# Small attention stages: denominators from the context matmul, sorted by DMA, weighed on GpSimd, projected two steps later

## What is computed

```python
q = (layernorm(x) @ Wq.T + bq).reshape(B, S, 16, 8).transpose(0, 2, 1, 3)
k = (ctx @ Wk.T + bk).reshape(B, S, 16, 8).transpose(0, 2, 1, 3)
v = (ctx @ Wv.T + bv).reshape(B, S, 16, 8).transpose(0, 2, 1, 3)
scores = jnp.einsum('bhqd,bhkd->bhqk', q, k) / jnp.sqrt(8.0)
attn = softmax(where(mask == 0, -1e9, scores), axis=-1)
ctx = jnp.einsum('bhqk,bhkd->bhqd', attn, v).transpose(0, 2, 1, 3).reshape(B, S, 128)
x = x + tanh(g) * (ctx @ Wo.T + bo)
```

## Time and profile before

| | |
|---|---|
| Median of 3 runs | 1778.14 us |
| Lowest and highest | 1774.27 and 1782.25 us |
| Span of the profiled execution | 1775.3 us (its total time is not given apart) |
| TensorE busy in the span | 1625.8 us, 92% |
| VectorE, ScalarE, GpSimd busy | 62%, 52%, 31% |
| Layer 0's attention | about 17 to 226 us of the span |
| Layer 3's attention | about 1444 to 1650 us |

### The profile page before, as it was taken

The page is one execution under the profiler, slowest core; times in us unless marked ns, Lnnn a source line. Parts: engine busy times, 40 slices in busy tenths (PEclk is TensorE's granted clock), DMA queues, the critical chain, the costliest instruction groups (busy, mean ns, idle before and its releaser), DMA issues. The chain is left out here.

```text
span 1775.3 us, 50142 instructions
## 1 busy us (share of the span) xinstructions
PE 1625.8 (92%) x19432; PEld 1110.8 (63%) x19432; DVE 1092.4 (62%) x2384; ACT 924.1 (52%) x2277; POOL 547.2 (31%) x968
## 2 busy tenths in 40 slices
PE   3999989899999999987987799979999978999898
PEld 1666654577777777764775456646777755666454
DVE  4677767566666666645156788862223236778686
ACT  3666526455656565533444566534334346665354
POOL 3455309333333332310211345300000015543672
PEclk9999999999999999989999899979999999999999
DMA  7433040000000000010103434110000035330000
GB/s 180 124 103 97 4 122 1 10 7 5 7 8 5 8 8 5 2 48 0 48 0 81 115 104 116 31 37 1 1 0 0 0 79 150 100 91 18 7 19 25
DMA packets 103135, 78.25 MB, mean 44 GB/s; under 512 B 17168, under 2 KB 99856, under 8 KB 102928
## 3 DMA queue, kind: packets, MB, share of 16 engines
q1 hardware_dynamic: 96032, 73.03, 15.4%
q10 hardware_dynamic: 6896, 2.32, 0.7%
HBM read 22.88 MB, written 2.10 MB: 14 GB/s over the span
## 5 line engine op out<-in xcount | busy, mean ns | idle before, releaser
L990 DVE TENSOR_REDUCE neg_max<-scores 128x8 f32<-128x1024 f32 x192 | 233.8, 1219 | 72.5 <-PE scores L649 33.2
L2068 POOL TENSOR_TENSOR probs<-probs,inverse 128x512 f32<-128x512 f32 x128 | 133.3, 1041 | 315.2 <-DVE inverse L2273 315.0
L2207 ACT ACTIVATE probs<-scores,neg_max 128x128 f32<-128x128 f32 x512 | 180.7, 388 | 5.3 <-DVE neg_max L2265 5.3
L872 ACT ACTIVATE probs<-turned 128x1024 bf16<-128x1024 f32 (+1 forms) x128 | 131.1, 1024 | 85.8 <-PE turned L672 85.7
L1726 ACT ACTIVATE hidden_f<-hb_f,b_f 128x512 f32<-128x512 f32 x128 | 88.0, 687 | 128.8 <-PE hb_f L1672 128.5
L1681 PEld LDWEIGHTS yb_f<-w_f,hidden_f 128*128 128x128 f32 x1024 | 119.2, 192 | 14.8 <-issue 14.8
L2198 ACT ACTIVATE heads_t<-heads 128x512 f32<-128x512 f32 x64 | 38.2, 597 | 166.8 <-PE heads L2133 166.8
L489 POOL TENSOR_TENSOR k_all<-k_all,k_parts 128x512 f32<-128x512 f32 x24 | 27.8, 1158 | 312.9 <-ACT k_parts L798 312.9
L1681 PE MATMUL yb_f<-w_f,hidden_f 128*128 128x128 f32 x1024 | 119.3, 275 | 0.0
L2207 ACT ACTIVATION_READ_ACCUMULATOR probs<-scores,neg_max 128x1 f32 x512 | 116.9, 228 | 0.0
L1672 PE MATMUL hb_f<-xn_all_f,w_f 128*128 (+1 forms) x256 | 116.8, 600 | 0.0
(11 more groups left out here) (340 smaller groups left out, 3820.9 us busy)
## 6 DMA issues: line engine op xcount, KB each, us to landing
k_rep<-k_parts SPq DMA_DIRECT2D x144, 128.0 KB, 2.5
q_rep<-q_parts SPq DMA_DIRECT2D x129, 128.0 KB, 2.5
ctx_t<-in_ctx_t_dram SPq DMA_DIRECT2D x24, 256.0 KB, 3.8
conv_weights_or_copies<-k_parts SPq DMA_DIRECT2D x32, 128.0 KB, 2.5
conv_weights_or_copies<-q_parts SPq DMA_DIRECT2D x32, 128.0 KB, 2.5
w_f<-in_L_ffn_W_dram SPq DMA_DIRECT2D x16, 256.0 KB, 3.2
x_state<-in_x_dram SPq DMA_DIRECT2D x4, 512.0 KB, 7.8
ctx_t<-in_ctx_t_dram SPq DMA_DIRECT2D x16, 128.0 KB, 2.1
```

The source lines that it names most:

```text
L872: nc.scalar.activation(probs[:, b % 2, pair, :], turned[:, :], ACT.Exp, **bias).then_inc(s["exp_done"], 1)
L990: v.tensor_reduce(neg_max[:, b % 2, 8 * pair:8 * pair + 8], scores[pair][:, :].rearrange("p (h k) -> p h k", k=S), axis=X_AXIS, op=ALU.max ...
L2068: nc.gpsimd.tensor_tensor(p4, p4, inverse[:, n % 2, CH * h:CH * h + CH].unsqueeze(2).to_broadcast([P, CH, S]), ALU.mult).then_inc(s["prob_ ...
L2207: last = nc.scalar.activation(probs[:, n % 2, h, c * S:(c + 1) * S], scores[n % 2][:, i * S:(i + 1) * S], ACT.Exp, bias=neg_max[:, n % 2, ...
```

## The change

For layers 0 and 3 (not for layer 2):

- `v_pad` gets a column of ones beside each value column, written once in `setup`, and `values_apart` writes every second column. The 16 matmuls of `contexts` then give contexts in even rows and denominators in odd rows of a 128x256 result; `sums` is left out.
- ScalarE copies this result to SBUF (`copy_heads`, tile `both`) at the start of the next step.
- SP sorts its rows into contexts and denominators (`gather_heads`, tile `dense`, ring of three): four DMAs of 64 rows by 512 bytes per batch. The replications of a group, which stood together, are cut in two parts with a sort between.
- VectorE takes the reciprocal from `dense`, GpSimd multiplies (`weigh_heads`), and `project_out` and `add_result` come one step later than before. The loops of all engines run one step longer.
- `w_o` of layer 0 is loaded in the new order of rows, in eight pieces.

The core of the diff:

```diff
-        for j in range(4):
-            load(eng, t["w_o"][32 * j:32 * j + 32, :],
-                 arg[pre + "Wo"].rearrange("(g j e) n -> j g e n", g=QUADS, j=4)[j])
+            by_tile = arg[pre + "Wo"].rearrange("(h t j e) n -> h j t e n", h=2, t=2, j=4)
+            for half in range(2):
+                for j in range(4):
+                    first = 64 * half + 16 * j
+                    load(eng, t["w_o"][first:first + 2 * DK, :], by_tile[half, j])
...
+            def gather_heads(b):
+
+                sp.wait_ge(s["both_done"], b + 1)
+                wait(sp, s["heads_ready"], b - DENSE + 1)
+                for half in range(2):
+                    rows = slice(64 * half, 64 * half + 64)
+                    for odd in range(2):
+                        sp.dma_start(dense[rows, b % DENSE, odd, :], both[odd:P:2, b % 2, half * S:half * S + S]) \
+                            .then_inc(moved[b % DENSE], 16)
...
+            for b in range(NB + 1):
+                if b > 0:
+                    gather_heads(b - 1)
+                if b % GB == 0 and b // GB + 2 < NG:
+                    c = b // GB + 2
+                    sp.wait_ge(s["st_done"], 8 * (c - 2))
+                    replicate_keys(c, 0)
+                    replicate_keys(c, 1)
+                    replicate_queries(c, 0)
+                if b % GB == 1 and b // GB + 2 < NG:
+                    c = b // GB + 2
+                    replicate_keys(c, 2)
+                    replicate_queries(c, 1)
+                    replicate_queries(c, 2)
+                    if c + CR - 1 < NG:
+                        load_context(c + CR - 1)
...
+            def weigh_heads(b):
+                if not real(b):
+                    return
+                pool.wait_ge(s["inv_done"], b + 1)
+                wait(pool, s["y_done"], b - 1)
+                p.tensor_tensor(heads_t[:, b % 2, :], dense[:, b % DENSE, 0, :], inverse[:, b % 2, :], ALU.mult) \
+                    .then_inc(s["heads_ready"], 1)
...
+                if not select:
+                    wait(pe, s["both_done"], b - 1)
+                    wait(pe, s["x_done"], b - 2)
+                    for u in range(QUADS):
+                        half, first = u // 2, APART * u - 2 * DK * (u % 2)
+                        for j in range(4):
+                            last = nc.tensor.matmul(heads[b % 2][32 * j:32 * j + 32, half * S:half * S + S],
+                                                    v_pad[:, b % 2, first + 32 * j:first + 32 * j + 32],
+                                                    probs[:, b % 2, half, (u % 2 * 4 + j) * S:(u % 2 * 4 + j + 1) * S],
+                                                    start=(u % 2 == 0), stop=(u % 2 == 1), skip_group_check=True)
+                    last.then_inc(s["sums_done"], 1)
+                    return
...
-            for b in range(-AHEAD, NB):
+            def copy_heads(b):
+                if not real(b) or select:
+                    return
+                act.wait_ge(s["sums_done"], b + 1)
+                if b >= 2:
+                    act.wait_ge(moved[(b - 2) % DENSE], MOVED * ((b - 2) // DENSE + 1))
+                nc.scalar.activation(both[:, b % 2, :], heads[b % 2][:, 0:2 * S], ACT.Copy).then_inc(s["both_done"], 1)
+
+            for b in range(-AHEAD, NB + 1):
+                copy_heads(b - 1)
...
+                if not select:
+                    dve.wait_ge(moved[b % DENSE], MOVED * (b // DENSE + 1))
+                    wait(dve, s["heads_ready"], b - 1)
+                    v.reciprocal(inverse[:, b % 2, :], dense[:, b % DENSE, 1, :]).then_inc(s["inv_done"], 1)
+                    return
```

More of the change, by code:

```diff
@@ L379, in attention_small @@
                  "shift_ready st_done exp_done sums_done inv_done heads_ready y_done x_done bq_ready mask_ready chain "
-                 "high_done rest_done mid_done").split()
+                 "high_done rest_done mid_done both_done").split()
         s = {n: sem(n) for n in names}
+        moved = [sem(f"moved{i}") for i in range(DENSE)]
         s_done, max_done = (s["s0_done"], s["s1_done"]), (s["max0_done"], s["max1_done"])
@@ L425, in values_of, with result_of @@
             return value_group(c).rearrange("p (u j e) -> p u j e", j=4, e=DK)
+        def result_of(b):
+            return heads[b % 2 if select else (b + 1) % 2][:, 0:D]
         def unit(t, u):
@@ L463, in _ @@
                     replicate_queries(0, 0)
-            for c in range(1, NG):
-                wait(sp, s["st_done"], 8 * (c - 2))
-                for part in range(3):
-                    replicate_keys(c, part)
-                for part in range(3):
-                    replicate_queries(c, part)
-                if c + CR - 1 < NG:
-                    load_context(c + CR - 1)
+            if select:
+                for c in range(1, NG):
+                    wait(sp, s["st_done"], 8 * (c - 2))
+                    for part in range(3):
+                        replicate_keys(c, part)
+                    for part in range(3):
+                        replicate_queries(c, part)
+                    if c + CR - 1 < NG:
[9 more added lines that the diff above has]
+                            .then_inc(moved[b % DENSE], 16)
+            for part in range(3):
+                replicate_keys(1, part)
+            for part in range(3):
+                replicate_queries(1, part)
+            load_context(CR)
+            for b in range(NB + 1):
[12 more added lines that the diff above has]
+                    replicate_queries(c, 2)
+                    if c + CR - 1 < NG:
+                        load_context(c + CR - 1)
         @block.gpsimd
@@ L524, in _ @@
                     low_of("q", c, q_all, q_parts)
-            for b in range(-AHEAD - 1, NB):
+            def weigh_heads(b):
[5 more added lines that the diff above has]
+                    .then_inc(s["heads_ready"], 1)
+            for b in range(-AHEAD - 1, NB if select else NB + 2):
                 if real(b + 1):
@@ L598, in _ @@
                 values(c)
+            if mask == "keys":
+                pe.wait_ge(s["consts"], 1)
             if mask is not None:
-                pe.wait_ge(s["consts"], 1)
                 pe.wait_ge(s["mask_ready"], 1)
@@ L706, in sums @@
             def sums(b):
-                if not real(b):
+                if not real(b) or not select:
                     return
@@ L725, in project_out @@
                 pe.wait_ge(s["heads_ready"], b + 1)
-                nc.tensor.matmul(heads[b % 2][:, 0:D], heads_t[:, b % 2, :], w_o[:, :], start=True, stop=True) \
+                if not select:
+                    pe.wait_ge(s["both_done"], min(b + 2, NB))
+                nc.tensor.matmul(result_of(b), heads_t[:, b % 2, :], w_o[:, :], start=True, stop=True) \
                     .then_inc(s["y_done"], 1)
-            for b in range(-AHEAD, NB + 1):
+            for b in range(-AHEAD, NB + (1 if select else 2)):
                 todo = first_fills(b)
@@ L1008, in add_result @@
                 xb = cols(st.x, b, D)
-                v.scalar_tensor_tensor(out=xb, in0=heads[b % 2][:, 0:D], scalar=gate, in1=xb, op0=ALU.mult,
+                v.scalar_tensor_tensor(out=xb, in0=result_of(b), scalar=gate, in1=xb, op0=ALU.mult,
                                        op1=ALU.add).then_inc(s["x_done"], 1)
@@ L1016, in statistics @@
                 v.bn_stats(cols(st.stats, b, 6), cols(st.x, b, D))
-            for b in range(-AHEAD, NB + 2):
+            late = 1 if select else 2
+            for b in range(-AHEAD, NB + late + 1):
                 if select:
                     choose_start(b)
-                add_result(b - 2)
+                add_result(b - late - 1)
                 maximum(b + AHEAD, 0)
-                statistics(b - 2)
+                statistics(b - late - 1)
                 if not select and (b + 10) % 4 == 0 and TQ0 <= (b + 10) // 4 < NG:
@@ L1027, in _ @@
                     choose_middle(b)
-                normalise_heads(b - 1)
+                normalise_heads(b - late)
                 maximum(b + AHEAD, 1)
```

60 lines of the change are left out of this document (35 added, 25 removed).

## The result

The changed kernel takes 1798.68 us (median of 4 runs, 1794.46 to 1800.38), the kernel before in the same session 1776.2 us (4 runs, 1774.12 to 1782.25). The ratio is 1.0119, 95% interval 1.0097 to 1.014: slower by 1.2%, 22 us. I had forecast no change that can be told (1774.5 us); the result lies in the range, in the case of the rival that SP's queue becomes the bound.

A forecast was written before the change was run, and what follows sets the result against it. ScalarE's exponential and shift copy were taken as next limit behind TensorE, VectorE as the path in some steps; -4.0 - 7.0 - 2.1 + 3.6 + 4.4 + 1.5 = -3.6 us gave 1774.5 us, range 1764 to 1808 us.

The forecast's parts named there:

- the rival that SP's queue becomes the bound: SP's DMA queue: sorts at 0.65 us each land late, VectorE waits; about +31 us, 1809 us; chance 0.22.
- the term of +3.6 us for late sorts: SP's queue, layers 0 and 3: one late sort a group costs 0.3 us, in six groups of each layer.
- the point of decision: Issue price per sort, about 0.44 us, from which twelve times the loss equals the 7.2 us gained.
- my walk from 95.54: SP's issues through one layer 0 group, sorts at 0.40 us: last sort lands at 114.6 us, 0.5 us late.
- TensorE absorbs ... some 0.35 us: Of a late reciprocal, TensorE absorbs what the split maxima have to spare before ScalarE's chain, some 0.35 us.
- The sums: Layers 0 and 3: removed matmuls save 0.16 and 0.28 us a step over 25 steps each, -4.0 and -7.0 us.
- A: Half of a loop step, between two additions of the shifts on TensorE, holding the sums; 2.42 us before.
- The multiply on GpSimd: VectorE-bound steps, five a layer: VectorE saves 0.21 us each, -2.1 us; GpSimd has room for the multiply.
- The copy on ScalarE at nothing: The new copy out of PSUM, about 0.384 us, costs nothing, as ScalarE is idle in half B.
- half B: The other half of a loop step, holding the contexts and output projection; 2.31 us in a light layer 0 step.
- The ends: After the last contexts of layers 0 and 3: copy, issues, landing and multiply add 2.2 us each, +4.4 us.
- The start: SP's setup issues before layer 0: eight smaller w_o loads instead of four, +1.0 to +2.9 us, taken as +1.5.

The follow-up runs named there:

- cured kernel: Changed kernel with two sorting DMAs a batch instead of four and the key and query copies spread four a step: 1763.23 us, ratio 0.9928 to the kernel before.

## Why the prediction was wrong, point by point

**The step that failed** is the price of a sort's issue, and with it the term of +3.6 us for late sorts, which came to 29.7 us: "The new ones' issue cost is not in the trace ... I take 0.40, since the new ones are plain two-dimensional and have fewer rows." The sorts measured 0.60 us, 0.62 with the gap, and 0.7 in the mean. The row that was nearest was the other one, the copies from SBUF to SBUF of the earlier trace rows; the runs with neighbouring rows and with merged sorts show that neither pattern nor number of rows enters. I gave the point of decision as 0.44 us, and the measured price is far over it, so the rival's mechanism is what happened: reciprocal, maximum, split, transposes, L739.

**Its second half:** even 0.62 us was the median and not the price. My 0.75 us for a copy was nearly right as a mean, though not for the reason that the prediction gave (a full queue makes issues longer): of the eight copies in 5.99 us the first took 1.44 us and the others 0.60 to 0.62 us. At the medians (0.62 a sort, 0.635 a copy) my walk from 95.54 issues the last sort at 113.1 us, and it lands 1.9 us later at 115.0 us, 0.9 us late against the 114.1 us wanted. At the mean of the group shown above, 0.73 us each, it lands at 117.9 us, 3.8 us late. The loops lost (177.71 - 165.62) + (177.87 - 160.29) = 29.7 us, 2.5 us in each of twelve groups (31.9 and 2.7 us without the first two steps). And my walk starts every group with an empty queue, while SP needs some 24 us for what a group of 22.3 us (21.4 us in layer 3) gives it, so a delay isn't worked off before the copies end.

**"TensorE absorbs ... some 0.35 us":** this was priced for the path by the split maxima; what that path absorbs was not measured alone. The projection two steps behind, first in TensorE's queue, has no such slack: I had not listed it as queued behind the sort. 27.4 us of waits cost 29.7 us (31.9). With many short waits (the spread copies) some is absorbed: 29.1 us of waits, 16.6 us of loops (21.4 without the first two steps).

**The sums:** mechanism right, size too small. A ended at 2.12 and 2.00 us, not 2.26 and 2.14: I laid exponential and shift copy end to end with 0.03 us between, and they overlap by 0.10 us. The Trainium skill (ScalarE: Activation LUTs, What ACT_TABLE_LOAD costs) says that back-to-back activations overlap by about 93 ns; the rows above agree. I also counted 25 halves a layer where nearly all gain. With the multiply's share the cured loops gain 7.2 and 10.8 us, 18.0 together, against my 4.0 + 7.0 + 2.1 = 13.1. Without the first two steps, slow in that execution, they gain 9.1 and 13.1 us.

**The multiply on GpSimd:** "there is room for it" was right for the loops. Its worth was 5 us, not 2.1: VectorE saves the whole 0.39 us of a bound step, and 0.1 to 0.2 us in other halves.

**The copy on ScalarE at nothing:** right. Beyond the first two steps no half B of the cured kernel is longer than before. The Trainium skill's warning (TensorEngine Tiling (Array Packing), PSUM Bottleneck), which I had weighed at 6%, did not come true.

**The merging rule:** the Trainium skill's advice to merge small transfers (DMA: Bandwidth & Descriptors, Rules for kernel authors) was the warning that mattered. I had it at 3.6 us; two sorts instead of four were worth 26 us, and it was the issue that was saved, not the landing, which rose from 1.9 to 2.1 us.

**The ends:** +2.2 us each; the cured kernel shows +2.5 and +2.7, the changed one +3.0 and +4.3, the latter with a sort wait of 1.45 us in layer 3 and projections of 0.80 instead of 0.49 us at the lower clock (granted 0.50 from 1664.7 to 1665.7 us). **The start:** +1.5 taken, +2.5 measured at the first `ctx` load (19.40 against 16.88), within the bounds; eight `w_o` loads took 5.51 us, 0.69 each with the gaps.

**The rival's sum:** I priced it at +31 us. Put together from what was measured: loops -18.0, waits +29.7, start +2.3, tails +3.0 and +4.3 are +21.1 us (unrounded terms). Its size was too high, as the loss in a group was less (3.15 to 3.5 us taken, 2.5 measured) and the gains were larger than I took; the ends, dearer than I took, make up for a part of it; its kind was right, and I had given it 0.22.

## What to carry to other kernels

Before adding DMAs to a queue, add up its issues over one period of the loop, old and new, and compare the sum with the period. Take the price from the nearest kind (here SBUF to SBUF with SBUF to SBUF), and from a long row of issues divided by their number, not from the median of one: here 0.73 us against 0.60. In this kernel 33 issues in a period were too many and 25, spread, made nothing wait. If the queue is too full, take issues away and spread the bursts. Merging did it here; sorts on another engine's queue were not tried. Moving the consumers one step later only moved the wait.

## What the runs showed that I had not expected

- The issue of an SBUF-to-SBUF copy on SP's queue took 0.60 us for 32, 64 and 128 KB, with stepped or neighbouring rows; loads of small weights from DRAM took 0.29 to 0.43 us, most of the eight of `w_o` 0.62, the context loads 0.59, a plain store 0.372 us. What makes the difference stays open.
- About one issue in fifteen held SP's queue for 0.9 to 2.2 us, in the kernel before too. The median hides it, and it decides whether this queue keeps up.
- 27.4 us of waits in 16 places cost more than 29.1 us in 24 places. A total of waits is no measure of the loss.
- TensorE's granted clock fell to 0.92 with irregular waits (layer 3, 26 us of 147 idle) and was 1.00 with both cures, regular steps and 18 us idle. No run shows it as the cause of the waits: where they went, it came back.
